# Level 1 of a multi-scale convolution: valid columns only in the feature eviction, two attention pixels per PSUM bank

## Chip, core and metric

One Trainium2 (trn2) chip, one of its cores. The metric is the device time of one execution in microseconds (us), lower is better. The kernel computes in fp32; a matrix product is three TensorE passes on fp32r parts (high by high, high by low, low by high).

## What is computed

The input is `x` (8 images, 64 channels, 128x128). Layer 0, cut to what matters here:

```
x0 = group_norm(x)
feats = []
for i in range(4):                       # level i: y pooled by 2**i
    y = x0 if i == 0 else mean over 2**i x 2**i blocks of x0
    y = relu(conv3x3_dilated(y, ds_w3[i]) + ds_b3[i])
    feats.append(ds_w1[i] @ y + ds_b1[i])              # 1x1
def att(f):
    f_att, f_idt = f[:16 channels], f[16:]
    ker = taps per image from mean(f_att)               # 3x3, one per channel
    return fus_w @ concat(conv13x13(f_att) + conv3x3(f_att, ker), f_idt) + fus_b
x = x + fin_w @ (att(feats[0]) + sum of att(feats[i]) repeated 2**i times) + fin_b
```

Layer 1 adds a 3x3 and a 5x5 convolution of the normalised result. The change touches level 1 of layer 0 alone (`i == 1`, 64x64 pixels), which the kernel works off first.

## The kernel before

**Stages.** The program is a chain of blocks: level 1 (one image after the other, about 62 to 713 us of the span), levels 2 and 3, level 0, and layer 1. Inside level 1 each engine runs `body(i)` for image i; images 1 to 6 are one loop (`Fori(1, B - 1)`), images 0 and 7 are written out. Order comes from the program text of each engine and from counting semaphores alone.

**Layout.** The 64 rows are split into an upper and a lower half on partitions 0 to 63 and 64 to 127. The 16 attention channels are laid out by phase: a 2x4 block of pixels times 16 channels makes 128 partitions, so `fh1`/`fl1` (high and low part) hold 32 by 16 block positions plus a margin of zeros, and the 13x13 filter becomes 7x4 = 28 tiles of 128x128 weights. `PIX` lists the eight pixels (dr, dc) of a block.

**One image on TensorE** (`body` at L948 of the listing below): four chunks of the dilated convolution into `ps_main`; the 1x1 product of three chunks (`plain`, 512 columns each), evicted by VectorE into `z1`; the *feature product* (`fa_h`, 48 matmuls of 288 columns, into both banks of `ps_q`); the *large filter* (28 tiles, 84 matmuls of 512 columns into `ps_lk`, with small products for the taps and for the next image's statistics between them); the fourth `plain`; and the *attention output*: for each of the eight pixels, six matmuls of 256 columns (`ga_h`, `ga_l` on `lh1`, `ll1`) into one of the two banks of `ps_q`, which VectorE then adds into every fourth column of `z1`.

**Feature eviction.** When the feature product is done, ScalarE writes `fh1` from PSUM with the bias (L617, one operation per half of the rows, 16x17 columns on all 128 partitions). VectorE then writes the rest, PSUM plus bias minus `fh1`, into `fl1` (L864). One of the 17 columns is wrong on each half of the partitions (column 1 on 0 to 63, column 17 on 64 to 127), so GpSimd waits for both (`qfree`) and clears them with four small memsets (L538, L539), and then counts `f_z`. TensorE waits for `f_z` before the large filter. GpSimd's pooling of the next image's chunks 5 to 7 (`prep_chunk`) is behind this wait in its queue.

**Attention output.** `ps_q` has two banks. For pixel p TensorE waits until VectorE has freed bank p % 2 (`qfree`). VectorE's queue in this place holds, besides the eight additions (L899), the last `plain` eviction and the four pieces in which it normalises the next image (`norm`, L693): pieces 0 and 1 ahead of pixel 0, piece 2 behind pixel 0, piece 3 behind pixel 1. Each piece goes on to ScalarE (L576, `nh1`) and to GpSimd (L514, `nl1`), and the next image's convolution waits for GpSimd's piece.

**Counts.** `Q` is the number of times per image that a `ps_q` bank is filled: 6 plus 8 pixels. `store(i)` of the SyncE queue waits for the last one and writes `z1` out.

Of the kernel before, what the change touches and what calls it, by code (L numbers as in the profile page):

```python
# [20 lines left out]
F32 = mybir.dt.float32  # L21
F32R = mybir.dt.float32r
ALU = mybir.AluOpType
ACT = mybir.ActivationFunctionType
AX = mybir.AxisListType

P = 128
B, C, H, W = 8, 64, 128, 128
# [15 lines left out]
def slot(dr, dc):  # L44

    return (dc // 2) * 4 + dr * 2 + dc % 2
# [8 lines left out]
PIX = [(dr, dc) for dr in range(2) for dc in range(4)]  # L55
# [23 lines left out]
def conv_kernel(nc, x, w3t, w1t, w1, b3, b1, kgw1t, kgb1, kgw2, kgb2, lkt, fus, fusb, fint, finb,  # L79
# [8 lines left out]
    with ExitStack() as ctx:  # L88
# [20 lines left out]
        ps_main, ps_q = ps_all[:, 0:2, :], ps_all[:, 2:4, :]  # L109
# [19 lines left out]
        b1a = mb("b1a", [P, LEVELS])  # L129
# [31 lines left out]
        def alone(eng):  # L161
            eng.sem_inc(passed, 1)


        def product(pe, o, wh, wl, xh, xl, first, last):

            pe.matmul(o, wh, xh, start=first, stop=False, skip_group_check=True)  # L167
            pe.matmul(o, wh, xl, start=False, stop=False, skip_group_check=True)  # L168
            return pe.matmul(o, wl, xh, start=False, stop=last, skip_group_check=True)  # L169
# [127 lines left out]
        ga_h = sb("ga_h", [P, 8 * P + C], F32R, stack=st1)  # L297
        ga_l = sb("ga_l", [P, 8 * P + C], F32R, stack=st1)
# [13 lines left out]
        with ExitStack() as st:  # L312
            def s1(name):
                return sem("p1_" + name, st)

            D1, S1, N1 = DIL[1], SIDE[1], half[1]
            NB1, NQ1 = N1 // 2, S1 // 4
# [8 lines left out]
            fh = sb("fh1", [P, N1 + 6, NQ1 + 4], F32R, stack=st)  # L326
            fl = sb("fl1", [P, N1 + 6, NQ1 + 4], F32R, stack=st)
# [80 lines left out]


            QF, QL, QY = 3, 5, 6  # L410
            Q = QY + 8

            pieces = [(0, 8 + 2 * D1)] + [(8 * k + 2 * D1, 8 * k + 8 + 2 * D1) for k in range(1, NCH)]
            xc_full = [s1("xc_full0"), s1("xc_full1")]
# [13 lines left out]
            r_h = s1("r_h")  # L428
            r_l = s1("r_l")
            f_h = s1("f_h")  # L430
            f_z = s1("f_z")
            sums = Steps(s1("sums"), 1)
            pooled_s, chain, hdn_s, ker_s = s1("pooled"), s1("chain"), s1("hdn"), s1("ker")
            dyn = Steps(s1("dyn"), DSTEPS)
# [14 lines left out]
            with nc.Block() as block:  # L449
# [43 lines left out]
                def _(pool):  # L493
# [23 lines left out]
                    def body(i, last, first=False):  # L517
                        pool.wait_ge(n_l, NCH * (i + 1))
                        alone(pool)
                        for k in range(NCH):  # L520
                            pool.wait_ge(r_h, NCH * i + k + 1)
                            r = slice(8 * k, 8 * k + 8)
                            pool.tensor_tensor(rl[:, r, 2:2 + S1],
                                               rf[:, k % 2, :].rearrange("p (r c) -> p r c", c=S1),
                                               rh[:, r, 2:2 + S1].bitcast(F32), ALU.subtract).then_inc(r_l, 1)
                            for c in prep_at(k, last):
                                prep_chunk(i + 1, c)
                        if first:
                            pool.wait_ge(s_hi, 8)
                            for dr, dc in PIX:  # L530
                                filter_low(dr, dc)
                            pool.wait_ge(s_lo, 8)
                            pool.wait_ge(s_base, 8)

                        pool.wait_ge(qfree, 2 + Q * i + QL)
                        alone(pool)
                        for t in (fh, fl):
                            pool.memset(t[0:C, 3:3 + N1, 1:2].bitcast(F32), 0.0).then_inc(f_z, 1)  # L538
                            pool.memset(t[C:P, 3:3 + N1, 1 + NQ1:2 + NQ1].bitcast(F32), 0.0).then_inc(f_z, 1)  # L539
                        pool.wait_ge(f_z, 4 * (i + 1))  # L540
                        alone(pool)
                        if not last:
                            for c in range(NX - 3, NX):
                                prep_chunk(i + 1, c)
                            prep_rest(i + 1)
                            norm(i + 1)
# [25 lines left out]
                def _(act):  # L572
# [14 lines left out]
                    def body(i, last, first=False):  # L587
# [25 lines left out]
                        for hf in range(2):  # L613
                            act.wait_ge(qful, Q * i + QF + hf + 1)
                            p0 = 3 + NB1 * hf
                            ps = ps_q[:, 1 - hf, 0:NB1 * (NQ1 + 2)].rearrange("p (n q) -> p n q", q=NQ1 + 2)
                            act.activation(fh[:, p0:p0 + NB1, 1:NQ1 + 2], ps[:, :, 0:NQ1 + 1], ACT.Identity,  # L617
                                           bias=b1a[:, 1:2]).then_inc(f_h, 1)
                        chain_act(act, i, 1, chain, hdn_s)
                        if not last:  # L620
                            group_stats_act(act, stats, i + 1, root)
# [42 lines left out]
                def _(dve):  # L664
# [152 lines left out]
                    def body(i, last, first=False):  # L817
# [42 lines left out]
                        for hf in range(2):  # L860
                            dve.wait_ge(f_h, 2 * i + hf + 1)
                            p0 = 3 + NB1 * hf
                            ps = ps_q[:, 1 - hf, 0:NB1 * (NQ1 + 2)].rearrange("p (n q) -> p n q", q=NQ1 + 2)
                            dve.scalar_tensor_tensor(fl[:, p0:p0 + NB1, 1:NQ1 + 2], ps[:, :, 0:NQ1 + 1],  # L864
                                                     b1a[:, 1:2], fh[:, p0:p0 + NB1, 1:NQ1 + 2].bitcast(F32),
                                                     ALU.add, ALU.subtract).then_inc(qfree, 1)
                        chain_pooled_dve(dve, i, ((1, 1),), pooled_s, chain)
                        if not last:
                            for c in range(NX - 3, NX):
# [21 lines left out]
                        if not last:  # L891
                            norm(i + 1, 0)
                            norm(i + 1, 1)
                        for p, (dr, dc) in enumerate(PIX):
                            dve.wait_ge(qful, Q * i + QY + p + 1)
                            if p == 0:
                                dve.wait_ge(qfree, 2 + Q * i + QY)
                            v = z1[:, dr::2, dc::4]
                            dve.tensor_tensor(v, v, ps_q[:, p % 2, 0:NB1 * NQ1].rearrange("p (n q) -> p n q", q=NQ1),  # L899
                                              ALU.add).then_inc(qfree, 1)  # L900
                            if p < 2 and not last:
                                norm(i + 1, 2 + p)
# [33 lines left out]
                def _(pe):  # L936
# [9 lines left out]
                    def body(i, last, first=False):  # L946
# [22 lines left out]
                        for j, (dr, dc) in enumerate(PIX):  # L969
                            a = 112 - ATT * slot(dr, dc)  # L970
                            for hf in range(2):
# [3 lines left out]
                                             fa_h[w], fa_l[w], rh[v], rl[v], j == 0, j == 7)  # L975
                                if j == 7:
                                    mm.then_inc(qful, 1)
                        pe.wait_ge(f_z, 4 * (i + 1))
                        pe.wait_ge(l_l, i + 1)
                        if first:  # L980
                            pe.wait_ge(s_hi, 8)
# [10 lines left out]
                        pe.wait_ge(l_l, i + 2)  # L992
                        if first:
                            pe.wait_ge(a_g, NA_G)
                        for p, (dr, dc) in enumerate(PIX):
                            pe.wait_ge(qfree, Q * i + QY + p + 1)
                            o = ps_q[:, p % 2, 0:NB1 * NQ1]
                            for hf in range(2):
                                g = slice(slot(dr, dc) * P + C * (1 - hf), slot(dr, dc) * P + C * (1 - hf) + P)
                                m = slice(hf * NB1 * NQ1, (hf + 1) * NB1 * NQ1)  # L1000
                                mm = product(pe, o, ga_h[:, g], ga_l[:, g], lh[:, m], ll[:, m], hf == 0, hf == 1)
                            mm.then_inc(qful, 1)


# [1964 lines left out]
```

## Time and profile before

| | |
|---|---|
| three runs | 2984.34, 2985.78, 2985.86 us, median 2985.78 |
| the profiled execution | 2986.26 us, its span 2984.5 us |
| TensorE busy | 2673.4 us, 90% of the span |
| VectorE, ScalarE, GpSimd busy | 2175.6, 1042.2, 627.9 us |
| mean granted TensorE clock | 0.933 of full speed |

The span runs from the first to the last instruction; what lies around it in the execution is 1.76 us. A busy time is the union of an engine's instructions, and a matmul's recorded duration overlaps the next one's, so what a stage costs is read from start times, not from durations. The granted clock is 1.00 at 2.4 GHz and 0.50 at 1.2 GHz.

### The profile page before, as it was taken

To read this page: it belongs to the slowest core of one execution; us is meant where nothing else is said; L and a number is where in the kernel's file an instruction comes from. 1 tells how busy PE (TensorE), PEld (TensorE's weight loads), DVE (VectorE), ACT (ScalarE), POOL (GpSimd) and SP (SyncE) were. 2 spreads that over 40 slices of the span, in tenths; PEclk is the share of its full clock that TensorE was granted. 3 is DMA by queue.
4 is the path that set the end of the run, shared out by engine and by line. 5 is a ranking of instruction groups with operands and counts; after the bars stand their busy time and mean duration, and the time that the engine had idled before them with its cause. 6 is when DMAs were issued, how large, how long until landed. Compare 5 with 4: busy or idle time off the path is not lost. (4 is left out here: it accounts for less than half of the span.)

```text
span 2984.5 us, 39118 instructions
## 1 busy us (share of the span) xinstructions
PE 2673.4 (90%) x12262; PEld 2146.1 (72%) x12262; DVE 2175.6 (73%) x3003; ACT 1042.2 (35%) x1605; POOL 627.9 (21%) x692
## 2 busy tenths in 40 slices
PE   3799999985999699999999599989985999999998
PEld 2666676764888588888888477767764777777776
DVE  4544344455454589888888779998876999999998
ACT  1111111110111098889889422222212232333332
POOL 5443344412221234444444200000001000000000
PEclk9899999987888699999999799999987999999999
DMA  6122222211000399999998223343342332323332
GB/s 120 42 71 72 72 72 72 72 30 33 6 20 12 61 203 217 219 219 216 219 219 207 99 89 131 145 157 144 115 161 118 95 114 90 119 90 119 91 113 63
DMA packets 288702, 338.04 MB, mean 113 GB/s; under 512 B 24816, under 2 KB 243824, under 8 KB 274288
## 3 DMA queue, kind: packets, MB, share of 16 engines
q1 hardware_dynamic: 277184, 332.76, 41.3%
q10 hardware_dynamic: 11440, 4.28, 0.9%
q8 instruction: 44, 0.72, 0.1%
q14 instruction: 34, 0.28, 0.0%
HBM read 211.60 MB, written 122.62 MB: 112 GB/s over the span
## 5 line engine op out<-in xcount | busy, mean ns | idle before, releaser
L167 PE MATMUL ps_all<-vh,u_h 128*128 128x512 f32 x960 | 384.9, 401 | 28.8 <-DVE vl L2739 28.1
L169 PE MATMUL ps_all<-vh,u_l 128*128 128x512 f32 x960 | 383.5, 400 | 0.0
L168 PE MATMUL ps_all<-vl,u_h 128*128 128x512 f32 x960 | 382.9, 399 | 0.0
L2648 ACT ACTIVATE vh<-rt,gn 128x528 fp32r<-128x528 f32 x192 | 130.4, 727 | 446.2 <-DVE rt L2716 319.7
L167 PE MATMUL ps_all<-vh,t_h 128*128 128x512 f32 x576 | 231.7, 402 | 24.3 <-DVE vl L1794 24.2
L167 PEld LDWEIGHTS ps_all<-vh,u_h 128*128 128x128 f32 x960 | 181.0, 189 | 82.4 <-issue 35.9
L168 PE MATMUL ps_all<-vl,t_h 128*128 128x512 f32 x576 | 229.6, 399 | 0.0
L169 PE MATMUL ps_all<-vh,t_l 128*128 128x512 f32 x576 | 229.4, 398 | 0.0
L169 PEld LDWEIGHTS ps_all<-vh,u_l 128*128 128x128 f32 x960 | 181.0, 189 | 46.2
L168 PEld LDWEIGHTS ps_all<-vl,u_h 128*128 128x128 f32 x960 | 181.3, 189 | 45.5
L167 PE MATMUL ps_all<-nh,w3h 128*128 128x512 f32 (+1 forms) x396 | 161.1, 407 | 35.4 <-POOL nl L1171 27.9
L1633 POOL TENSOR_TENSOR zr<-zr,z 128x256 f32<-128x256 f32 x128 | 104.8, 839 | 354.7 <-DMA xr<-in_x 354.7
L668 DVE BATCH_NORM_STATS2 stat<-xc 128x6 f32<-128x512 f32 x128 | 81.4, 681 | 130.0 <-DMA xc<-in_x 130.0
L168 PE MATMUL ps_all<-nl,w3h 128*128 128x512 f32 (+1 forms) x396 | 158.3, 400 | 0.0
L169 PE MATMUL ps_all<-nh,w3l 128*128 128x512 f32 (+1 forms) x396 | 158.2, 400 | 0.0
L1637 POOL TENSOR_TENSOR xr<-xr,zr 128x1024 f32<-128x1024 f32 x64 | 152.9, 2389 | 5.0
L167 PEld LDWEIGHTS ps_all<-vh,t_h 128*128 128x128 f32 x576 | 108.8, 189 | 51.2 <-issue 25.9
L1722 ACT ACTIVATE rp_h<-yt,b3p 128x1024 fp32r<-128x1024 f32 x64 | 142.7, 2230 | 0.0
L2275 DVE TENSOR_TENSOR xq<-xq,ps_all 128x512 f32<-128x512 f32 x128 | 130.8, 1091 | 12.6 <-PE ps_all L169 12.4
L167 PE MATMUL ps_all<-ch,w_h 128*128 128x512 f32 x280 | 120.1, 429 | 17.8 <-DVE cl L2195 9.9
L2739 DVE SCALAR_TENSOR_TENSOR vl<-rt,gn,vh 128x1056 fp32r<-128x1056 f32 x96 | 127.5, 1328 | 3.0 <-ACT vh L2648 3.0
L169 PEld LDWEIGHTS ps_all<-vh,t_l 128*128 128x128 f32 x576 | 108.7, 189 | 27.9
(394 smaller groups left out, 6797.4 us busy)
## 6 DMA issues: line engine op xcount, KB each, us to landing
xc<-in_x SPq DMA_DIRECT2D x128, 256.0 KB, 3.9
xr<-in_x SPq DMA_DIRECT2D x128, 256.0 KB, 4.2
x_layer<-xr SPq DMA_DIRECT2D x64, 512.0 KB, 2.7
xq<-x_layer SPq DMA_DIRECT2D x32, 1024.0 KB, 4.9
x_layer<-xq SPq DMA_DIRECT2D x32, 1024.0 KB, 3.9
out<-ot SPq DMA_DIRECT2D x64, 512.0 KB, 5.2
xw<-in_x SPq DMA_DIRECT2D x112, 288.0 KB, 5.1
xw<-x_layer SPq DMA_DIRECT2D x16, 1152.0 KB, 8.7
```

The source lines that it names most:

```text
L167: pe.matmul(o, wh, xh, start=first, stop=False, skip_group_check=True)
L168: pe.matmul(o, wh, xl, start=False, stop=False, skip_group_check=True)
L169: return pe.matmul(o, wl, xh, start=False, stop=last, skip_group_check=True)
L668: dve.bn_stats(stat[:, 2 * c + e, :], xc[:, c % 2, 4 * e:4 * e + 4, :].rearrange("p a b -> p (a b)")).then_inc(bn_done, 1)
L1633: pool.tensor_tensor(v, v, zz, ALU.add).then_inc(z_a, 1)
L1637: pool.tensor_tensor(v, v, zz.to_broadcast([P, 512, 2]), ALU.add).then_inc(x_z, 1)
L1722: act.activation(phases(rp_h, t % 2), yt[:, :, :].rearrange("p n (q d) -> p n q d", d=4), ACT.Relu, bias=b3p[:, 0:1]).then_inc(r_h, 1)
L2275: dve.tensor_tensor(v, v, ps_all[:, 3 + dc, :].rearrange("p (n q) -> p n q", q=32), ALU.add).then_inc(qfree, 1)
L2648: act.activation(vh[:, v % 2, n, :, :].rearrange("p a b -> p (a b)"), rt[:, n, :, :].rearrange("p a b -> p (a b)"), ACT.Identity, scale=gn ...
L2739: dve.scalar_tensor_tensor(vl[:, v % 2, 2 * c:2 * c + 2, :, :].rearrange(f), rt[:, 2 * c:2 * c + 2, :, :].rearrange(f), gn1[:, bass.ds(i, ...
```

## The change

The feature eviction writes only the valid 16 columns of each half of the partitions: four operations of 64 partitions on ScalarE and four on VectorE per image, where two and two of 128 partitions stood. GpSimd's four memsets, its two waits around them and the semaphore `f_z` are gone; TensorE waits for VectorE's count (`qfree`) instead. The attention output puts two pixels of one row (256 columns each) into a bank of `ps_q`, so there are four fillings and four additions of 512 columns instead of eight of 256. The matmuls are the same ones. Normalisation pieces 2 and 3 stay behind the first and the second addition.

```diff
-            Q = QY + 8
+            Q = QY + 4
+            inner = ((slice(0, C), 2), (slice(C, P), 1))
...
-                        pool.wait_ge(qfree, 2 + Q * i + QL)
-                        alone(pool)
-                        for t in (fh, fl):
-                            pool.memset(t[0:C, 3:3 + N1, 1:2].bitcast(F32), 0.0).then_inc(f_z, 1)
-                            pool.memset(t[C:P, 3:3 + N1, 1 + NQ1:2 + NQ1].bitcast(F32), 0.0).then_inc(f_z, 1)
-                        pool.wait_ge(f_z, 4 * (i + 1))
-                        alone(pool)
...
-                            act.activation(fh[:, p0:p0 + NB1, 1:NQ1 + 2], ps[:, :, 0:NQ1 + 1], ACT.Identity,
-                                           bias=b1a[:, 1:2]).then_inc(f_h, 1)
+                            for hp, c0 in inner:
+                                ins = act.activation(fh[hp, p0:p0 + NB1, c0:c0 + NQ1], ps[hp, :, c0 - 1:c0 - 1 + NQ1],
+                                                     ACT.Identity, bias=b1a[hp, 1:2])
+                            ins.then_inc(f_h, 1)
...
-                            dve.scalar_tensor_tensor(fl[:, p0:p0 + NB1, 1:NQ1 + 2], ps[:, :, 0:NQ1 + 1],
-                                                     b1a[:, 1:2], fh[:, p0:p0 + NB1, 1:NQ1 + 2].bitcast(F32),
-                                                     ALU.add, ALU.subtract).then_inc(qfree, 1)
+                            for hp, c0 in inner:
+                                ins = dve.scalar_tensor_tensor(fl[hp, p0:p0 + NB1, c0:c0 + NQ1],
+                                                               ps[hp, :, c0 - 1:c0 - 1 + NQ1], b1a[hp, 1:2],
+                                                               fh[hp, p0:p0 + NB1, c0:c0 + NQ1].bitcast(F32),
+                                                               ALU.add, ALU.subtract)
+                            ins.then_inc(qfree, 1)
...
-                        for p, (dr, dc) in enumerate(PIX):
+                        for p in range(4):
...
-                            v = z1[:, dr::2, dc::4]
-                            dve.tensor_tensor(v, v, ps_q[:, p % 2, 0:NB1 * NQ1].rearrange("p (n q) -> p n q", q=NQ1),
+                            dr, dc = PIX[2 * p]
+                            v = z1[:, dr::2, :].rearrange("p n (q s) -> p n q s", s=4)[:, :, :, dc:dc + 2]
+                            dve.tensor_tensor(v, v, ps_q[:, p % 2, :].rearrange("p (s n q) -> p n q s", s=2, q=NQ1),
                                               ALU.add).then_inc(qfree, 1)
...
-                        pe.wait_ge(f_z, 4 * (i + 1))
+                        pe.wait_ge(qfree, 2 + Q * i + QL)
...
-                        for p, (dr, dc) in enumerate(PIX):
+                        for p in range(4):
                             pe.wait_ge(qfree, Q * i + QY + p + 1)
-                            o = ps_q[:, p % 2, 0:NB1 * NQ1]
...
+                            for e in range(2):
+                                dr, dc = PIX[2 * p + e]
+                                o = ps_q[:, p % 2, e * NB1 * NQ1:(e + 1) * NB1 * NQ1]
```

**First place: VectorE in the attention output of images 1 to 6** (`z1` is the sum, `pl1` the next image, `ll1` the low part of the filter's result). Before:

```order
L699 COPY z1<-ps_all 128x512 [waits p1_qful]
L693 TENSOR_SCALAR pl1<-pl1,coef1 128x1152
L693 TENSOR_SCALAR pl1<-pl1,coef1 128x512
L895 REGISTER_ALU
L897 REGISTER_ALU [waits p1_qful]
L899 TENSOR_TENSOR z1<-z1,ps_all 128x16x16 [waits p1_qfree]
L693 TENSOR_SCALAR pl1<-pl1,coef1 128x512
L899 TENSOR_TENSOR z1<-z1,ps_all 128x16x16 [waits p1_qful]
L693 TENSOR_SCALAR pl1<-pl1,coef1 128x512
L895 REGISTER_ALU
L899 TENSOR_TENSOR z1<-z1,ps_all 128x16x16 [waits p1_qful]
L895 REGISTER_ALU
L899 TENSOR_TENSOR z1<-z1,ps_all 128x16x16 [waits p1_qful]
```

With the change:

```order
L696 COPY z1<-ps_all 128x512 [waits p1_qful]
L690 TENSOR_SCALAR pl1<-pl1,coef1 128x1152
L690 TENSOR_SCALAR pl1<-pl1,coef1 128x512
L895 REGISTER_ALU
L897 REGISTER_ALU [waits p1_qful]
L900 TENSOR_TENSOR z1<-z1,ps_all 128x16x16x2 [waits p1_qfree]
L690 TENSOR_SCALAR pl1<-pl1,coef1 128x512
L900 TENSOR_TENSOR z1<-z1,ps_all 128x16x16x2 [waits p1_qful]
L690 TENSOR_SCALAR pl1<-pl1,coef1 128x512
L895 REGISTER_ALU
L900 TENSOR_TENSOR z1<-z1,ps_all 128x16x16x2 [waits p1_qful]
L895 REGISTER_ALU
L900 TENSOR_TENSOR z1<-z1,ps_all 128x16x16x2 [waits p1_qful]
```

Both normalisation pieces that stood behind pixels 0 and 1 now stand behind pixels 0 and 1 together and behind pixels 2 and 3 together; four additions are gone, and each of the four that are left has 16x16x2 columns.

**Second place: GpSimd between the low part of the last chunk (`rl1`) and the pooling of chunk 5.** Before:

```order
L521 REGISTER_ALU
L523 TENSOR_TENSOR rl1<-rf1,rh1 128x8x64 [waits p1_r_h]
L535 ISA
L538 MEMSET fh1 64x32 [waits p1_qfree]
L539 MEMSET fh1 64x32
L538 MEMSET fl1 64x32
L539 MEMSET fl1 64x32
L303 TENSOR_TENSOR pl1<-xc 128x256 [waits p1_f_z,p1_xc_full1]
```

With the change:

```order
L523 REGISTER_ALU
L525 TENSOR_TENSOR rl1<-rf1,rh1 128x8x64 [waits p1_r_h]
L303 TENSOR_TENSOR pl1<-xc 128x256 [waits p1_xc_full1]
L304 REGISTER_ALU
L306 TENSOR_TENSOR pl1<-pl1,xc 128x256 [waits p1_p_acc]
```

The wait for VectorE and the four memsets are gone; the pooling follows at once.

**Third place: VectorE in the feature eviction.** Before:

```order
L864 SCALAR_TENSOR_TENSOR fl1<-ps_all,b1a,fh1 128x16x17 [waits p1_f_h]
L861 REGISTER_ALU
L864 SCALAR_TENSOR_TENSOR fl1<-ps_all,b1a,fh1 128x16x17 [waits p1_f_h]
L268 ISA
L272 TENSOR_SCALAR pooled<-ps_all,b1a 16x1 [waits p1_chain]
```

With the change:

```order
L862 SCALAR_TENSOR_TENSOR fl1<-ps_all,b1a,fh1 64x16x16 [waits p1_f_h]
L862 SCALAR_TENSOR_TENSOR fl1<-ps_all,b1a,fh1 64x16x16
L858 REGISTER_ALU
L862 SCALAR_TENSOR_TENSOR fl1<-ps_all,b1a,fh1 64x16x16 [waits p1_f_h]
L862 SCALAR_TENSOR_TENSOR fl1<-ps_all,b1a,fh1 64x16x16
L268 ISA
L272 TENSOR_SCALAR pooled<-ps_all,b1a 16x1 [waits p1_chain]
```

Two operations on 128 partitions became four on 64; ScalarE's L617 becomes four in the same way. VectorE waits for ScalarE twice, as before, each time now for a pair.

## Rows read from the trace of the kernel before

**Rows 1.** Stretches of five attention outputs: start:end, length, busy times, PEclk, DMA.

```profile
137.35:146.56 9.21, 6.88 (x48) 6.07 (x49) 8.24 (x12) 2.87 (x4) 6.14 (x4) 1.00 0.01 2
215.15:225.53 10.38, 8.11 (x48) 7.50 (x49) 8.17 (x12) 2.87 (x4) 6.11 (x4) 0.84 0.00 0
451.02:460.16 9.14, 6.87 (x49) 6.05 (x50) 8.19 (x12) 2.87 (x4) 6.13 (x4) 1.00 0.00 0
607.95:618.33 10.38, 8.11 (x49) 7.50 (x50) 8.18 (x12) 2.87 (x4) 6.12 (x4) 0.84 0.00 0
696.00:704.02 8.02, 8.01 (x48) 7.47 (x48) 4.96 (x8) 0.00 (x0) 0.00 (x0) 0.80 0.00 0
```

**Rows 2.** Who waited for whom, level 1: total us, times, longest us.

```profile
PE ps_all L167 <- POOL fl L539: 19.8, 8, 2.6
PE ps_all L167 <- DVE z L899: 15.7, 14, 1.6
```

**Rows 3.** Timeline of TensorE, attention output of image 1: start us, us, instruction.

```profile
215.15 0.38 PE L167 MATMUL ps_all<-lh,ga_h 128*128 128x256 f32 x1 [0.86 <-DVE ll L889]
216.56 0.28 PE L169 MATMUL ps_all<-lh,ga_l 128*128 128x256 f32 x1
217.46 0.39 PE L167 MATMUL ps_all<-lh,ga_h 128*128 128x256 f32 x1 [0.62 <-DVE z L899]
221.06 0.39 PE L167 MATMUL ps_all<-lh,ga_h 128*128 128x256 f32 x1 [1.63 <-DVE z L899]
```

**Rows 4.** Timeline of VectorE, the same stretch.

```profile
216.78 0.62 DVE L899 TENSOR_TENSOR z<-z,ps_all 128x256 f32<-128x256 f32 x1
217.31 0.53 DVE L693 TENSOR_SCALAR pl<-pl,coef 128x512 f32<-128x512 f32 x1
218.31 2.14 DVE L693 TENSOR_SCALAR pl<-pl,coef 128x512 f32<-128x512 f32 x1
220.38 1.17 DVE L899 TENSOR_TENSOR z<-z,ps_all 128x256 f32<-128x256 f32 x2
```

**Rows 5.** GpSimd there: its timeline, and the first piece's group (us busy, mean ns).

```profile
217.71 6.11 POOL L514 TENSOR_TENSOR nl<-pl,nh 128x1152 fp32r<-128x1152 f32 x4 [17.61 <-ACT nh L576]
L514 POOL TENSOR_TENSOR nl<-pl,nh 128x1152 fp32r<-128x1152 f32 x8 | 19.7, 2465 | 124.9 <-ACT nh L576 124.9
```

**Rows 6.** VectorE groups kept apart by shape: count, us busy, mean ns of one.

```profile
L2275 DVE TENSOR_TENSOR xq<-xq,ps_all 128x512 f32<-128x512 f32 x128 | 130.8, 1091 | 12.6 <-PE ps_all L169 12.4
L899 DVE TENSOR_TENSOR z<-z,ps_all 128x256 f32<-128x256 f32 x64 | 39.5, 628 | 16.7 <-PE ps_all L169 15.7
L889 DVE TENSOR_TENSOR ll<-ps_all,lh 128x512 fp32r<-128x512 f32 x8 | 5.5, 692 | 5.7 <-ACT lh L623 5.5
L780 DVE TENSOR_TENSOR xc<-xc,room 128x256 f32<-128x256 f32 x6 | 2.6, 426 | 0.2
```

**Rows 7.** Line L278, reads PSUM with strides of 4 or 8 elements: ns min/median/max.

```profile
L278 DVE TENSOR_TENSOR kerr<-ps_all,kb x12: 168/169/196, 119.0 to 962.7; 128x9 f32<-128x9 f32 x8, 128x36 f32<-128x36 f32 x4
L278 DVE TENSOR_TENSOR kerr_all<-ps_all,kb x1: 220/220/220, 1678.1 to 1678.1; 128x72 f32<-128x72 f32 x1
```

**Rows 8.** Timeline of the feature eviction of image 2, three engines.

```profile
262.17 0.87 ACT L617 ACTIVATE fh<-ps_all,b1a 128x272 fp32r<-128x272 f32 x2 [9.72 <-PE ps_all L169]
262.70 0.91 DVE L864 SCALAR_TENSOR_TENSOR fl<-ps_all,b1a,fh 128x272 fp32r<-128x272 f32 x2 [7.09 <-ACT fh L617]
264.61 0.51 PE L167 MATMUL ps_all<-fh,lk_h 128*128 128x512 f32 x1 [2.46 <-POOL fl L539]
```

**Rows 9.** Timeline, operations on half of the partitions: VectorE L711, ScalarE L1744.

```profile
68.39 0.86 DVE L711 COPY room<-ps_all 64x256 f32<-64x256 f32 x2
1106.59 1.32 ACT L1744 ACTIVATE ft<-ps_all,b1a 128x64 f32<-128x64 f32 x5
```

**Rows 10.** Stretches of the large filter, images 0 and 2, columns as in rows 1.

```profile
106.03:135.67 29.64, 29.64 (x109) 21.64 (x109) 11.06 (x22) 1.74 (x3) 9.84 (x12) 0.84 0.10 24
264.61:291.85 27.24, 27.24 (x109) 19.64 (x109) 11.31 (x22) 1.74 (x3) 9.99 (x12) 0.94 0.10 25
```

More of the change, by code:

```diff
@@ L430, in conv_kernel @@
             f_h = s1("f_h")
-            f_z = s1("f_z")
             sums = Steps(s1("sums"), 1)
@@ L994, in body @@
                             pe.wait_ge(a_g, NA_G)
-                        for p, (dr, dc) in enumerate(PIX):
+                        for p in range(4):
                             pe.wait_ge(qfree, Q * i + QY + p + 1)
-                            o = ps_q[:, p % 2, 0:NB1 * NQ1]
[L998 to L1001, printed above, removed]
+                            for e in range(2):
+                                dr, dc = PIX[2 * p + e]
+                                o = ps_q[:, p % 2, e * NB1 * NQ1:(e + 1) * NB1 * NQ1]
+                                for hf in range(2):
+                                    g = slice(slot(dr, dc) * P + C * (1 - hf), slot(dr, dc) * P + C * (1 - hf) + P)
+                                    m = slice(hf * NB1 * NQ1, (hf + 1) * NB1 * NQ1)
+                                    mm = product(pe, o, ga_h[:, g], ga_l[:, g], lh[:, m], ll[:, m], hf == 0, hf == 1)
                             mm.then_inc(qful, 1)
```

## The prediction

> **What bounds the kernel now.** I read the busy table first: TensorE works 90% of the span, VectorE 73%. Level 1 is a chain of TensorE stages, one image after the other, so only what TensorE waits for, or runs at the lower clock for, counts there. Next I cut the span into stretches from one stage's first matmul to the next stage's [rows 1]. The attention output takes 9.21 us in image 0, 9.14 in image 4, and 10.36 to 10.38 in the five others before the last; 48 matmuls are busy for only 6.9 to 8.1 us of it. The table of waits names the reasons [rows 2]: 15.7 us for the addition into `z1` and 19.8 us, 8 times, for GpSimd's last memset ahead of the large filter. These are the two places that the change touches.
>
> **The output stage in time.** TensorE starts at 215.15, and its twelfth matmul at 216.56, 0.12 us apart after the first; then it is idle 0.62 us before 217.46 and 1.63 us before 221.06 [rows 3]. VectorE shows why [rows 4]: the additions start at 216.78, and the fourth normalisation piece, started at 218.31, lasts 2.14 us where the third lasted 0.53. GpSimd began its own pieces at 217.71, the first of 2.465 us, so until 220.18 [rows 5]; VectorE's piece ends 0.27 us after that. TensorE has run two pixels ahead and stands. The clock follows: 0.84 in the stretches of 10.4 us, 1.00 in the two short ones [rows 1], that is, part of such a stretch at 1.2 instead of 2.4 GHz, after TensorE had been idle for 1.63 us.
>
> **Change 1: two pixels per bank.** The matmuls are the same; a bank now holds 12 of them, 1.43 us. New is the addition of 512 columns. Its price isn't in the trace, so I bound it. Dense, 512 columns with PSUM in cost 692 ns and 256 cost 426; every fourth column costs 628 for 256 and 1091 for 512 [rows 6]. So a column costs 1.04 ns dense and 1.81 ns with the stride of four. The new operation takes two neighbours out of each four columns of `z1` (dense pairs) but steps 256 columns in PSUM for each element. Between 0.69 and 1.09 us, then. The PSUM side: the tap operation reads PSUM with a stride of 4 or 8, and 9 columns take 169 ns, 72 take 220, that is 0.8 ns per column [rows 7], so strides in PSUM cost nothing there. That is the nearest row for the read, and it lets me take the lower end, 0.70 us; 1.09 is the other end.
>
> With 0.70 us image 1 goes like this. TensorE: pairs 0 and 1 from 215.15 to 218.0 without a wait (both banks are free), pair 2 needs addition 0. VectorE: addition 0 from 216.88 (12th matmul's end, 216.84) to 217.58; piece 2 from 217.50, 0.2 us ahead of GpSimd's 217.71, to 218.03; addition 1 from 218.24 to 218.94; piece 3 from 218.85, held by GpSimd to 220.45 as before; additions 2 and 3 from 220.38 and 221.1. So pair 2 starts at 218.0 and pair 3 at 219.45, both with their bank free, and the held piece no longer stops TensorE. The stage takes 1.41 us plus 37 steps of 0.119, 5.81 us, and the next convolution starts at 220.96, behind GpSimd's first piece (220.18), so it needn't wait. Seven images before: 9.21 + 9.14 + 5 times 10.37 = 70.2; after: 40.7; **29.5 us saved**. Image 7 has no normalisation and runs at 0.80 of the clock in 8.02 us [rows 1]; there TensorE's 48 matmuls bound it already, and I count 0.4 us: behind a wait the next matmul starts 0.2 instead of 0.12 us later (1.41 us for the first 11 steps [rows 3]), and four waits are gone.
>
> **Change 2: the feature eviction.** Now [rows 8]: ScalarE 262.17 to 263.04, VectorE 262.70 to 263.61, then GpSimd, and TensorE at 264.61, idle 2.46 us. So the clearing costs 1.0 us, and it goes. In its place stand four operations of 256 columns per engine. ScalarE: 16 columns fewer in 487 ns, about 475; in a row of mixed halves its operations start 0.25 apart for 0.31 long [rows 9], so mine start 0.38 to 0.42 apart: pairs end 0.90 and 1.70 us after the product. VectorE: 480 ns each; L864's two start 0.41 apart, but the two copies of 64x256 on different halves take 0.86 for two of 0.41, no overlap [rows 9]. Start 0.94, four times 0.50, end 2.92; TensorE at about 3.0 instead of 2.46. With overlap it would be 2.65. **I lose 0.5 us per image, 4 us**; bounds 0.2 and 0.65 (all eight operations end to end where they depend), 1.6 to 5.2 us in all. The Trainium skill (VectorE: DVE Perf Modes, section on two Vector instructions with no wait between them) says that an instruction whose operands start in another quarter of the partitions than the last one's is held until that one has finished; by it the loss is the 0.5 us, by L864's spacing alone 0.2.
>
> The longer pause can also cost clock. After today's pause the large filter runs at 0.94 of the clock in image 2 and at 0.84 in image 0, which takes 29.64 against 27.24 us [rows 10]. I count no change in the sum, and 2.4 us per image as the bound of one more low stretch.
>
> **Edits at nothing.** GpSimd's wait and memsets gone: pooling of chunks 5 and 6 moves about 10 us forward, under the feature product; VectorE's PSUM work isn't slowed by it (additions at 220.38 run beside GpSimd, 1.17 for two). Chunk 7's load needs VectorE's statistics of chunk 5, which come 1.5 us later, and GpSimd's pooling, which comes earlier; the load was bound by the latter, so it lands sooner. `chain_pooled_dve` starts 1.5 us later and the gelu's table load 0.8, before large-filter tile 4 asks for them some 4 us on. SyncE's `store` waits for the last addition, and that one ends about as far behind the next convolution's start as now. If that cover went, the next image's chunks would load later by as much; VectorE waits for them anyway.
>
> **Sum.** 29.5 + 0.4 - 4.0 = 25.9 us, from the profiled 2986.26 us (0.5 above the median of the runs shown): **2960.4 us**.
>
> **Rivals.**
> *Piece 2 is caught too.* If the addition takes more than 0.83 us, piece 2 comes behind 217.71 and is held to 220.4; addition 1 then ends at 221.1 to 221.5, pair 3 starts there, 2.0 us idle, and the stage ends at 223.0 (full clock) to 224.1. Saved 1.4 to 2.5 us per image, 10 to 18; less 4: 2972 to 2980, say **2977**. For it: the 1.81 ns rows and a margin of 0.2 us; against it: rows 7. The Trainium skill (Advanced Engine Details and Errata, Memory Cachelines) says that SBUF wants two hits in each line of 16 bytes, which the new pairs give, and PSUM pairs of neighbours (8 bytes), which the new read doesn't give; of PSUM it says this for matmuls. The first half agrees with the 1.81 ns at stride four; by the second the addition costs about 1.09 us and this rival comes true. Rows 7 speak against it for strides up to 8 columns; for 256 no row does.
> *Nothing measurable.* That, and one more low stretch of half the bound (1.2 us) in each large filter: 2977 + 10 = 2987.
> *Slower.* The pause of 3 us leaves the large filter at 1.2 GHz longer, in every image. Place: its first tiles. It decides from 29.9 / 8 = 3.7 us per image, pause included; for 0.2% more, 4.5 us. Image 0 shows 2.4 us more than image 2, so twice that with 0.5 would give 5.3 per image: 2986.3 - 30 + 42 = **2998**. Against it: 2.4 is the most that any row shows.
>
> **How the numbers follow.** The first case 70%, the caught piece 21%, nothing measurable 5%, slower 4%. Under 0.2% (6 us) is about what can't be told from no change here. Faster 0.91, same 0.05, slower 0.04. The first case alone reaches from 2954 (eviction at 0.2, a low stretch or two less) to 2972 (eviction at 0.65 and a low stretch more in half the images). To leave out no more than 2 in 10 I go to 2979, over most of the second case.
>
> **What would show it.** Right: additions of 512 at about 0.70 us; an output stage of 5.8 us at clock 1.00; no TensorE wait for the addition in images 0 to 6; the fourth piece still at 2.1 us; TensorE idle 3.0 us before the large filter, now for VectorE; large filters at 27 to 28 us. Wrong: additions over 0.83 us with a third piece of 2 us; large filters over 29 us; a wait of the next convolution for GpSimd's first piece.

## The result

| | kernel before | changed kernel |
|---|---|---|
| runs | 2984.34 to 2987.47 us | 2955.59, 2957.86, 2961.58, 2962.12 us |
| median | 2985.82 us | **2959.72 us** |
| ratio of the medians, 95% interval | | 0.9914, 0.9900 to 0.9927 |
| the profiled execution, its span | 2986.26, 2984.5 us | 2955.59, 2953.6 us |
| mean granted clock | 0.933 | 0.935 |
| TensorE, VectorE, ScalarE, GpSimd busy | 2673.4, 2175.6, 1042.2, 627.9 us | 2657.0, 2159.9, 1050.4, 619.9 us |

The change gains 26.1 us where 25.9 were predicted. The rest of this document shows that the output stage came as predicted, that the eviction's term was wrong, and that the closeness of the two totals is in part luck: the same kernel run again (changed_again) gained 21.4 us.

**The output stage.** Stretches of image 1, 2 and 7 in the trace of the changed kernel, columns as in [rows 1]:

```profile
210.40:216.25 5.85, 5.85 (x48) 5.85 (x49) 5.62 (x8) 2.51 (x4) 3.22 (x2) 1.00 0.00 0
285.20:291.05 5.85, 5.85 (x48) 5.85 (x49) 5.61 (x8) 2.51 (x4) 3.22 (x2) 1.00 0.00 0
670.84:676.85 6.01, 6.01 (x48) 5.81 (x48) 2.61 (x4) 0.00 (x0) 0.00 (x0) 1.00 0.00 0
```

In images 0 to 6 the stage takes 5.85 or 5.86 us, against 9.1 to 10.4 in [rows 1], and TensorE is busy for all of it. The timeline of VectorE and GpSimd in image 1 (L690 the normalisation, L900 the addition of a pair), to be laid beside [rows 4, 5]:

```profile
210.86 1.33 DVE L690 TENSOR_SCALAR pl<-pl,coef 128x1152 f32<-128x1152 f32 x2
212.22 0.69 DVE L900 TENSOR_TENSOR z<-z,ps_all 128x512 f32<-128x512 f32 x1
212.83 0.55 DVE L690 TENSOR_SCALAR pl<-pl,coef 128x512 f32<-128x512 f32 x1
213.03 6.32 POOL L516 TENSOR_TENSOR nl<-pl,nh 128x1152 fp32r<-128x1152 f32 x4 [18.64 <-ACT nh L571]
213.57 0.69 DVE L900 TENSOR_TENSOR z<-z,ps_all 128x512 f32<-128x512 f32 x1 [0.20 <-PE ps_all L169]
214.18 1.81 DVE L690 TENSOR_SCALAR pl<-pl,coef 128x512 f32<-128x512 f32 x1
215.91 1.27 DVE L900 TENSOR_TENSOR z<-z,ps_all 128x512 f32<-128x512 f32 x2
```

The third piece starts at 212.83, 0.20 us ahead of GpSimd's 213.03, and lasts 0.55 us. The fourth is held for 1.81 us, and now nobody waits for it: the next convolution starts at 216.25 as TensorE runs through.

**The feature eviction.** Timeline of image 2, to be laid beside [rows 8]:

```profile
252.64 1.97 ACT L613 ACTIVATE fh<-ps_all,b1a 64x256 fp32r<-64x256 f32 x4 [9.47 <-PE ps_all L169]
253.65 2.00 DVE L862 SCALAR_TENSOR_TENSOR fl<-ps_all,b1a,fh 64x256 fp32r<-64x256 f32 x4 [7.57 <-ACT fh L613]
255.70 0.80 PE L167 MATMUL ps_all<-fh,lk_h 128*128 128x512 f32 x1 [3.09 <-DVE fl L862]
```

VectorE's four stand 0.50 us apart, as predicted, but so do ScalarE's (1.97 us for four), and as VectorE waits for a pair of them it can only start 1.0 us after the product. TensorE is idle 3.08 or 3.09 us instead of 2.46 (in image 0, 3.15 instead of 2.61).

**Where the time went,** from the first matmul of each stage in the two timelines, level 1 summed over its images, in us:

| stage | before | changed | difference | predicted |
|---|---|---|---|---|
| attention output, images 0 to 6 | 70.2 | 41.0 | -29.2 | -29.5 |
| attention output, image 7 | 8.0 | 6.0 | -2.0 | -0.4 |
| feature product and the pause behind it | 71.9 | 76.9 | +5.0 | +4.0 |
| large filter | 221.5 | 223.6 | +2.1 | 0 |
| 1x1 stages with their waits | 67.0 | 66.1 | -0.8 | 0 |
| convolution of image 0 | 28.4 | 28.7 | +0.3 | 0 |
| all ahead of level 1's first matmul | 55.5 | 52.9 | -2.6 | 0 |
| all behind level 1 | 2252.5 | 2249.2 | -3.4 | 0 |

With 0.3 us less wait behind image 7 these make the 30.9 us between the two spans. The last two rows, 6.0 us together, are not the change's: in a second profile of the same changed kernel (below) they were 54.9 and 2254.7 us. The median stands 4.1 us above the profiled execution, and 26 us is what the runs give.

### The profile page after: what moved, and what is told of

Same layout as the page of the kernel before. It is cut to its first block and busy times, and to the rows that moved or that the text cites. A ratio compares the mean times of both kernels' runs of the same rounds, so it can differ in the third digit from the quotient of the medians.

```text
span 2953.6 us, 39022 instructions
## 1 busy us (share of the span) xinstructions
PE 2657.0 (90%) x12262; PEld 2136.0 (72%) x12262; DVE 2159.9 (73%) x2987; ACT 1050.4 (36%) x1621; POOL 619.9 (21%) x660
## 5 line engine op out<-in xcount | busy, mean ns | idle before, releaser
L167 PE MATMUL ps_all<-vh,u_h 128*128 128x512 f32 x960 | 385.2, 401 | 29.2 <-DVE vl L2742 28.2
L167 PE MATMUL ps_all<-fh,lk_h 128*128 128x512 f32 x224 | 109.0, 487 | 24.7 <-DVE fl L862 24.7
```

## The experiments

**Each half of the change alone.**

pairs_only: the kernel before with `Q = QY + 4`, the pair addition and the pair of pixels on TensorE, and the old eviction.

> The kernel before with two pixels per bank alone; feature eviction and clearing stay as they were. My theory: the two parts add. The output stages of images 0 to 6 take 5.85 us (as in the changed kernel), the pause ahead of the large filter stays at 2.46 us, and the time is about 5 us under the changed kernel's 2959.7 (0.63 us for each of 8 images): 2954.7. Rival, the clock answers for the difference: the longer pause of the changed kernel costs or gives clock in the large filter, so that this kernel differs from it by 0 to 2 us or by more than 8 us.

Measured: 2959.04 us (2957.07 to 2960.61), before 2985.51, ratio 0.9914 (0.9900 to 0.9927). That is 26.5 us (21.8 to 29.9), not 30.8. Stages 5.85 us, pauses 2.46, as expected; but the total is 0.7 us from the changed kernel's, which is what the rival asked for.

valid_only: the changed kernel with the output part of the diff taken back.

```diff
-            Q = QY + 4
+            Q = QY + 8
...
-                        for p in range(4):
+                        for p, (dr, dc) in enumerate(PIX):
```

> The changed kernel with one pixel per bank and eight additions again; the feature eviction writes valid columns only and nothing is cleared. My theory: 0.63 us longer pause in each of 8 images, so 2985.8 + 5 = 2991; output stages as before (9.2 and 10.4 us), pause 3.08 us, VectorE's four operations 0.50 apart. Rival, earlier pooling on GpSimd pays for the pause: 2986 or less.

Measured: 2985.44 us (11 runs), ratio 1.0004 (0.9995 to 1.0013): the eviction alone costs -1.5 to +3.9 us, and the 5 us expected lie outside, the prediction's 4.0 just so. Its trace has the pauses of 3.08 to 3.16 us (product and pause together 5.1 us longer than before over eight images). The rival's total fits, but not its cause: all seven later convolutions take 25.94 us as before, and the 1x1 stages only 1.0 us less. In this trace the time comes back in the output stages, here that of image 1:

```profile
215.17:224.38 9.21, 6.88 (x48) 6.07 (x49) 8.23 (x12) 2.87 (x4) 6.13 (x4) 1.00 0.00 0
```

Its program is that of [rows 1]'s 10.38, with the same waits (TensorE idle 0.69 and 1.61 us), but at full clock. Six of seven such stages take 9.21 or 9.22 us and run at full clock, where before two of seven did (9.21 and 9.14 us, with TensorE idle 1.61 and 1.62 us in them); their sum falls from 70.2 to 65.7. In pairs_only the large filters are longer instead: 225.4 us together against 221.5, one of them

```profile
254.50:282.56 28.06, 28.06 (x109) 20.28 (x110) 10.53 (x22) 1.74 (x3) 10.09 (x12) 0.90 0.10 25
```

at 0.90 where image 2 had 0.94 in [rows 10]. The two halves' totals do add (26.5 and 0.1 us against 26.1 together); what doesn't carry over to the total is the change of a stage's length. The eviction costs less than its 5.1 us, clear of the noise. The pairs gain 26.5 us where their stages show 29.8, which the interval just allows.

What the traces show behind this is the time at half clock (0.50, 1.2 GHz). Level 1 from its first matmul to its last, TensorE alone (busy time and matmuls, clock, DMA), in the kernel before, in pairs_only and in fill_pause (below):

```profile
55.50:704.02 648.52, 576.54 (x2604) 0.92 0.23 59
53.32:677.01 623.69, 566.52 (x2604) 0.92 0.24 62
55.77:651.52 595.75, 548.43 (x2604) 0.96 0.26 65
```

Summed from the same clock records, TensorE is at half clock for 102 us of level 1 before and for 102 in pairs_only, though no output stage of images 0 to 6 has any of it there; for 106 in valid_only, 99 in both profiles of the changed kernel, and 92 to 106 in all the others but two (51 in fill_pause, 164 in one_bank_first). So the stretches at half clock don't go with the idle time of one stage; they turn up in another one. Where they fall differs between executions of one program too: the large filters took 224.9 us together in by_partition's profile and 228.7 in that of by_partition_2, with medians 0.1 us apart. A difference of 2 to 4 us in the large filters between two single profiles is therefore no sign of what was changed.

**The addition's price.**

dense_read: `ps_q[:, p % 2, :].rearrange("p (n q s) -> p n q s", s=2, q=NQ1)` in the addition instead of `"p (s n q) -> p n q s"`.

> The changed kernel, but the addition of 512 columns reads its bank of PSUM in the order of the addresses instead of with a step of 256 columns for each element; the 512 sums therefore go to other columns of z1 than they should, and this part of the output is not the reference's. It prices the PSUM side of the addition alone. My theory: strides in PSUM cost VectorE nothing, the addition stays at 684 ns within 10. Rival (PSUM is read in pairs of neighbours): the strided read costs something, and the dense one is 50 to 200 ns shorter. The total is the changed kernel's 2959 to 2962 by both, since TensorE waits for no addition.

The group of the addition, level 1, first in the changed kernel's trace and then in this one's (us busy, mean ns):

```profile
L900 DVE TENSOR_TENSOR z<-z,ps_all 128x512 f32<-128x512 f32 x32 | 21.4, 684 | 5.2 <-PE ps_all L169 4.9
```

```profile
L900 DVE TENSOR_TENSOR z<-z,ps_all 128x512 f32<-128x512 f32 x32 | 21.3, 683 | 5.2 <-PE ps_all L169 5.0
```

684 against 683 ns: a step of 256 elements in PSUM costs VectorE nothing here, so what the prediction's second case feared from the PSUM side did not happen. The one run took 2961.53 us.

split_add:

```diff
-                            v = z1[:, dr::2, :].rearrange("p n (q s) -> p n q s", s=4)[:, :, :, dc:dc + 2]
+                            for e in range(2):
+                                v = z1[:, dr::2, dc + e::4]
...
+                            ins.then_inc(qfree, 1)
```

> The changed kernel, but each bank of two pixels is emptied by two additions of 256 columns in every fourth column of z1 instead of one of 512 in pairs of neighbours. An addition pair then costs about 1.17 us (two at 220.38 took 1.17) instead of 0.68. This is what the rival of the caught third piece asked for: the third normalisation piece comes behind GpSimd's start, is held to its first piece's end (2 us instead of 0.55), TensorE waits for the addition, and the output stage takes 7.9 to 8.9 us: 2 to 3 us more in each of 7 images, so 2974 to 2981. Rival, the bank of two pixels alone does it and the cheaper addition is worth little: stages of 5.9 to 6.5 us, 2960 to 2964.

Measured: 2984.59 us, ratio 0.9999 (0.9989 to 1.0008). Its output stage of image 1 and rows of its timeline, in which `...` stands for rows left out:

```profile
217.49:225.54 8.05, 6.29 (x48) 5.96 (x49) 8.02 (x10) 2.50 (x4) 4.94 (x3) 1.00 0.00 0
```

```profile
219.31 1.18 DVE L902 TENSOR_TENSOR z<-z,ps_all 128x256 f32<-128x256 f32 x2
220.13 4.94 POOL L516 TENSOR_TENSOR nl<-pl,nh 128x1152 fp32r<-128x1152 f32 x3 [20.52 <-ACT nh L571]
220.40 2.48 DVE L690 TENSOR_SCALAR pl<-pl,coef 128x512 f32<-128x512 f32 x1
...
224.00 0.39 PE L167 MATMUL ps_all<-lh,ga_h 128*128 128x256 f32 x1 [1.75 <-DVE z L902]
```

This is the rival of the caught piece, made true: the addition takes 1.18 us, the third piece comes 0.27 us behind GpSimd's start and is held 2.48 us, and TensorE stands 1.75 us. The stage takes 8.03 to 8.06 us, inside the expected 7.9 to 8.9, 2.2 more than 5.85 and 15 us in seven images. The total lies outside the expected 2974 to 2981, 10 us above the changed kernel and those 15. In this trace the large filters take 4.0 us more (227.6 together), the 1x1 stages 3.3 and image 7's output stage 1.6; the first is no more than two profiles of one program can differ by. Against the kernel before, the seven stages are still 13.9 us shorter (56.3 against 70.2) and the total is the same. So in the total the bank of two pixels by itself gains nothing that can be measured: all of the gain needs the addition of 684 ns, with which the third piece is 0.2 us ahead. This run makes the addition dearer and catches the piece at once; it doesn't tell the two apart.

**The pause.**

changed_again: no edit.

> The changed kernel itself, once more, as the partner of the three others on one chip. Its first profile had large filters of 27.3 to 29.5 us, with 3.4 to 9.2 us of each at half clock. Theory A (the clock takes back or gives back, and by the image's place in time): 2958 to 2962, output stages 5.85 and pauses 3.08 as before, but single large filters at other lengths. Theory B (a pause counts in full, the rest is fixed): the same large filters image by image within 0.1 us.

2962.07 us (2960.97 to 2964.10), 21.4 under the kernel before of that comparison (2983.47; 0.993, 0.9916 to 0.9944). Large filters of 27.3 to 28.1 us, 222.2 together, and image 0's 27.8 where the first profile had 29.5: theory A. The interval is a gain of 16.7 to 25.1 us, and the predicted 25.9 lies just outside it.

small_ops: both evictions in blocks of 8 rows, twice as many operations.

> The changed kernel with the feature eviction in eight operations of 128 columns on each engine instead of four of 256, so that the pause ahead of the large filter grows by about 1.2 us (0.4 of it on ScalarE, 0.8 on VectorE) to 4.3 us. Theory B, a pause counts in full: 8 times 1.2 = 10 us more than the changed kernel, 2969 to 2971. Theory A, the clock gives back a part of it: pauses of 4.3 us, but less time at half clock in the large filters (41.5 us over eight of them in the changed kernel), and 2960 to 2966.

Pause 3.90 us (I had expected 4.3), 2965.73 us: 3.7 us more than changed_again for 8 times 0.82 = 6.6 us of pause.

wait_each:

```diff
-                            ins.then_inc(f_h, 1)
+                                               ACT.Identity, bias=b1a[hp, 1:2]).then_inc(f_h, 1)
...
+                            for k, (hp, c0) in enumerate(inner):
+                                dve.wait_ge(f_h, 4 * i + 2 * hf + k + 1)
```

> The changed kernel, but VectorE waits for each of ScalarE's four operations of the feature eviction instead of for each pair. My theory is that ScalarE's halves follow each other 0.49 us apart without overlap and VectorE's 0.50 apart, so the pair wait alone delays VectorE by one operation: pause 3.08 - 0.5 = 2.58 us, 8 times 0.5 = 4 us less, 2955.7. Rival, two engines on the same PSUM bank slow each other or the semaphore of each operation costs 0.1 us: pause 2.8 to 3.1 us, 2958 to 2960.

Pause 2.61 us as by my theory, and yet 2961.80 us, no gain: large filters 227.1 us together, 3.5 more than in the changed kernel, within what two profiles of one program differ by.

by_partition: wait_each with `for hp` outside and `for hf` inside, on both engines.

> As wait_each, but both engines do the two operations on partitions 0 to 63 first and then the two on 64 to 127. My theory of the spacing, on VectorE from the two copies on different halves (0.86 us for two of 0.41, end to end), is that an operation is held only when its partitions begin elsewhere than the last one's: VectorE's second and fourth then start about 0.41 us after the one before, not 0.50, and the pause is 0.1 to 0.2 us shorter than in wait_each (2.61). Rival: the spacing is 0.49 to 0.50 in every order, since operations on 64 partitions never overlap, and the pause stays at 2.6 us. The total by either is within 3 us of wait_each's 2961.8.

The evictions of an image, wait_each first, then by_partition:

```profile
176.94 2.00 ACT L613 ACTIVATE fh<-ps_all,b1a 64x256 fp32r<-64x256 f32 x4 [10.03 <-PE ps_all L169]
177.45 2.02 DVE L861 SCALAR_TENSOR_TENSOR fl<-ps_all,b1a,fh 64x256 fp32r<-64x256 f32 x4 [7.08 <-ACT fh L613]
```

```profile
178.16 1.71 ACT L613 ACTIVATE fh<-ps_all,b1a 64x256 fp32r<-64x256 f32 x4 [9.93 <-PE ps_all L169]
178.67 1.78 DVE L861 SCALAR_TENSOR_TENSOR fl<-ps_all,b1a,fh 64x256 fp32r<-64x256 f32 x4 [7.14 <-ACT fh L613]
```

Four operations take 0.29 us less on ScalarE and 0.24 less on VectorE when neighbours in the queue lie on the same partitions; the pause is 2.42 us. The Trainium skill (VectorE: DVE Perf Modes, Two Vector instructions with no wait between them) tells this of VectorE, and the trace agrees; that ScalarE does the same is this case's number. 2958.77 us (2958.23 to 2959.19), 3.3 under changed_again for 8 times 0.66 = 5.3 us of pause; a second time 2958.85 us (by_partition_2, before 2983.42).

> by_partition once more, as the partner of fill_pause on one chip: pause 2.42 us, 2957 to 2961.

one_bank_first: wait_each with the loop over the halves outside that over the pixels in the feature product.

> As wait_each (VectorE waits for each operation of ScalarE), and TensorE finishes the feature product's first bank before it begins the second, so that half of the eviction lies under the second half of the product (about 3.2 us). The pause ahead of the large filter falls from 3.08 to about 1.6 us (ScalarE 0.5, VectorE 0.5 twice, and the starts). Theory B: 8 times 1.5 = 12 us less than the changed kernel, 2948. Theory A: the large filters take back a part, as in wait_each, where 0.5 us less pause brought nothing: 2953 to 2960.

2995.16 us, ratio 1.0036 (1.0022 to 1.0050): a clear miss. The pause did fall to 1.61 us, but the product takes 11.9 us instead of 6.5. Three microseconds of the product, TensorE alone (busy time and matmuls, clock, DMA), in the kernel before at low clock (image 1) and at full clock (image 2), and here (image 1):

```profile
177.40:180.40 3.00, 3.00 (x27) 0.51 0.29 74
256.00:259.00 3.00, 3.00 (x26) 1.00 0.19 49
```

```profile
176.40:179.40 3.00, 3.00 (x13) 0.50 0.06 16
```

With the two halves of the partitions taking turns, 26 or 27 matmuls fit in 3 us at either clock; one half after the other, 13 at half clock, half as many. So two matmuls on different halves run side by side. The Trainium skill (TensorE: Matmul & The Clock Gate, Part 3: Packing small matmuls) says that matmuls on different row groups overlap; the rows agree.

**Work in the pause.**

fill_pause: by_partition, and chunk 2's 1x1 product behind the feature product.

```diff
-            QF, QL, QY = 3, 5, 6
+            QF, QL, QY = 2, 4, 5
...
-                        for k in range(3):
+                        for k in range(2):
                             plain(i, k)
...
+                        plain(i, 2)
                         pe.wait_ge(qfree, 2 + Q * i + QL)
```

> by_partition, with the 1x1 product of chunk 2 (three matmuls, about 0.8 us) moved from ahead of the feature product into the pause behind it; it goes into a bank of ps_main that is free there, and VectorE evicts it in the course of the large filter. The feature product then waits for the eviction of chunk 1 instead of chunk 2, and starts 0.5 to 0.9 us earlier after the convolution, while the pause keeps its 2.42 us from the product's end to the large filter, with 0.8 us of it filled. Theory B, the stages' lengths count in full: 8 times 0.7 = 5.6 us less than by_partition, 2953. Theory A, the clock takes a part back in the large filters (in my runs so far a pause counted for some 0.6 of its length): 2954 to 2957. Rival: the last chunk's low part on GpSimd ends as late as the eviction did, so the product starts no earlier: 2958 to 2960.

fill_changed: the same move in the changed kernel.

> The changed kernel with its own order of the feature eviction (VectorE waits for pairs), and only the move of fill_pause: chunk 2's 1x1 product stands in the pause. It tells what fill_pause's 21.8 us under by_partition hang on. Theory C, the clock: three matmuls cut TensorE's idle time ahead of the large filter from 3.08 to about 2.15 us and keep it at work ahead of that; in fill_pause six large filters then ran at full clock throughout (26.12 us each) where by_partition's took 27.9 to 29.6. If work in the pause is what counts, the large filters take 26.1 to 26.9 us here too, though the idle time is nearly by_partition's 2.42 us; with stages 1 us shorter ahead of the product that gives 2938 to 2943. Theory D, the length of the idle time alone decides: at 2.15 us the large filters fall to half clock as in by_partition (27.3 to 29.5 us), and only the 8 us of the earlier product are left: 2952 to 2955.

| | time | before | ratio (95%) |
|---|---|---|---|
| by_partition_2 | 2958.85 | 2983.42 | 0.9912 (0.9898 to 0.9925) |
| fill_pause | **2937.07** | 2983.42 | 0.9842 (0.9828 to 0.9855) |
| fill_changed | 2956.92 | 2985.14 | 0.9904 (0.9887 to 0.9920) |

Stretches of image 2 (1x1 stage, feature product, what stands up to the large filter, large filter), columns as in [rows 1], for by_partition_2, fill_pause and (the last two alone) fill_changed:

```profile
243.11:247.43 4.32, 2.78 (x12) 1.53 (x10) 2.97 (x6) 0.78 (x2) 3.60 (x5) 1.00 0.29 79
247.43:253.91 6.48, 6.48 (x48) 5.60 (x48) 0.00 (x0) 0.00 (x0) 2.98 (x5) 0.74 0.13 33
253.91:256.34 2.43, 0.01 (x1) 0.00 (x0) 1.79 (x5) 2.30 (x5) 0.00 (x0) 0.74 0.00 0
256.34:284.40 28.06, 28.06 (x108) 20.34 (x109) 11.33 (x24) 2.41 (x4) 5.69 (x6) 0.90 0.10 25
```

```profile
236.36:239.71 3.35, 1.77 (x9) 1.04 (x7) 2.55 (x6) 0.78 (x2) 2.99 (x5) 1.00 0.21 53
239.71:246.12 6.41, 6.41 (x50) 5.61 (x48) 0.00 (x0) 0.00 (x0) 3.93 (x6) 0.73 0.31 82
246.12:248.62 2.50, 1.00 (x6) 0.49 (x4) 1.79 (x5) 2.31 (x5) 0.03 (x1) 1.00 0.00 0
248.62:274.74 26.12, 26.12 (x109) 18.72 (x109) 12.73 (x25) 2.40 (x4) 5.86 (x6) 1.00 0.11 26
```

```profile
249.49:252.66 3.17, 1.01 (x6) 0.49 (x4) 1.96 (x5) 2.99 (x5) 0.00 (x0) 0.99 0.00 0
252.66:281.39 28.73, 28.73 (x109) 20.94 (x109) 12.45 (x25) 1.95 (x4) 5.70 (x6) 0.88 0.09 24
```

fill_pause gains 21.8 us over by_partition_2, four times the 5.6 that its stages promised. The 1x1 stage is 1.0 us shorter, as expected; the rest is the large filter, 26.12 us in images 1 to 6 at a clock of 1.00 (26.11 in one), 211.0 us over all eight against 228.7. The profile is of the fastest of the five runs and the partner's of its second slowest, so these stages show more than the medians: 28.7 us between the two. I had expected at most 5.6 us, so both theories A and B failed on it. fill_changed shows that the work alone isn't enough: the same work in the pause, but TensorE idle 2.16 us ahead of the large filter instead of 1.49, and the large filter falls to 0.88 of the clock and takes 28.6 to 28.8 us in six of eight images. The two kernels differ in the order of the eviction as well, so that the idle time decides is argued, not shown. Its total is within 2 us of where theory D put it. fill_pause is the fastest version of this study, 22.7 us under the changed kernel's 2959.7 and 46.4 under the kernel before that ran beside it.

## Why the prediction was right, and where it was not

**The sum** of 25.9 us against 26.1 measured is right by cancellation. The halves alone give 26.5 and 0.1 us, where the steps had 29.9 and -4.0. The eviction's 4.0 is refuted (-1.5 to +3.9), the 29.9 stands at the edge of its interval (21.8 to 29.9). That the two differ by only 0.2 us is also luck of the runs: the same kernel gained 21.4 us the second time.

**Output stage: the mechanism was right.** The addition's price of 0.70 us, taken by the rows of L278 against the end of 1.09, measured 0.684. The walk through image 1, counted from the stage's start, against the timeline: addition 0 at 1.73 (measured 1.82), third piece 2.35 (2.43), GpSimd 2.56 (2.63), fourth piece 3.70 (3.78); the stage 5.81 (5.85). One step was off at no cost: the fourth piece was held to 5.59 us, not 5.30, and the last two additions came 0.3 us later, for which TensorE has nothing left to wait. The 29.5 us were 29.2. The 426 ns of [rows 6], read as a dense addition with PSUM in, are an addition within SBUF; the lower bound rests on the 692 ns and stands. The rival's mechanism and its stage of 7.9 us came true in split_add (addition 1.18 us, stage 8.05 us), its limit of 0.83 us was not tried, and its price was wrong: it named 2977 and the run gave 2984.6.

**Image 7: a term that depends on the clock.** It was 2.0, not 0.4 us: "TensorE's 48 matmuls bound it already" was true, but they ran at 0.80 of the clock before and at 1.00 now. In pairs_only, with the same output stage, it was 0.6 (7.45 us), so the 2.0 is not the change's alone.

**Feature eviction: the failed step.** "I lose 0.5 us per image, 4 us" holds two errors. The pause grew by 0.62 us, inside the bounds of 0.2 and 0.65, because ScalarE's halves stand 0.49 apart and not 0.38 to 0.42; I had taken the spacing of a mixed row [rows 9] on ScalarE and the held one only for VectorE. And the step from pause to time, taken as one to one, is wrong: valid_only has all of the longer pauses and costs 0 (-1.5 to +3.9).

**"I count no change in the sum" for the clock** left out that shorter output stages could send time at half clock elsewhere. In pairs_only the large filters took 3.8 us more, which by itself is no more than two profiles of one program differ by; that level 1 stays at half clock for 102 us in both kernels is the stronger sign. The prediction read 0.84 in the output stage as the effect of its 1.63 us of idle time; valid_only has 1.61 and stays at 1.00, and so did images 0 and 4 of the kernel before, with 1.61 and 1.62.

**Edits at nothing: held.** The pooling moved and no wait for it appeared. GpSimd now waits longer for its loads instead of for VectorE, off the path. *Nothing measurable* asked for the caught piece, which did not come, and 1.2 us more per image in the large filter; it was 0.26. *Slower* asked for 3.7 us per image, pause included; it was 0.9.

What stays open: what decides between 27.2 and 29.6 us in one large filter when the idle time ahead of it is 2.2 us or more. No two runs differ in the idle time alone below 2.6 us: fill_pause and fill_changed differ in it, but in the order of the eviction too, and they ran on different chips. Nor does a run show why the time at half clock in level 1 stays near 100 us.

## What to carry to other kernels

Price an idle time of TensorE by what the next long stage's granted clock does, not by its length: pauses between 2.2 and 3.9 us counted here for none to two thirds of their length, and between the two kernels with 2.16 and 1.49 us lay some 18 us in eight images (28.2 against 46.4 us gained, each against the kernel before that ran beside it). Sum the time at half clock over the whole level, too: if it is what it was, a stage that lost its own has passed it on. Before shortening an eviction that TensorE waits for, look for a small product that can stand in the pause. An operation of one engine that holds another's decides by who starts first, so write down both start times: an addition 0.5 us dearer, which turned a lead of 0.2 us into a lag, was the difference between 26 us and nothing measurable.

## What the runs showed of the hardware

- Large filter after TensorE's idle time ahead of it, image by image: 1.49 us, 26.12 us at clock 1.00 (six images of fill_pause; 27.3 and 27.0 at 0.94 in the outer two); 2.16 us, 26.8 to 28.8; 2.42 to 2.62 us, 26.8 to 29.6; 3.08 us, 26.9 to 29.6; 3.90 us, 27.5 to 29.0. Short idle time alone isn't enough: after 1.61 us in one_bank_first, behind a product at 0.50 of the clock, it took 27.5 to 29.4 us.
- Two ScalarE operations on different halves of the partitions stand 0.49 us apart; by_partition, with two of three steps staying on the same half, takes 1.71 instead of 2.00 us for four.
- Matmuls on 64 partitions that take turns between the halves: 27 in 3 us at clock 0.51 and 26 at 1.00. One half after the other: 13 at 0.50.
- Time at half clock in level 1, whose length is 596 to 659 us: 92 to 106 us in twelve of fourteen profiles, wherever TensorE's idle times lay; 51 us in fill_pause, 164 us in one_bank_first.
- VectorE's addition of 512 columns with a step of 1 KB in PSUM: 684 ns, in the order of the addresses 683 ns.
